# One attention and expert-routing layer on one core: softmax sums from a column of ones, a router maximum as a bias, and a new order of steps

## The reference

```python
h = _L0_tok_ref(x, ...)                  # gated recurrence: z, f, o from two-tap convolutions
h = h + _L0_attn_ref(_layernorm(h), ...) # attention to 39 offsets (0..32, 48, 64, 96, 128, 192, 256)
h = h + _L0_ffn_ref(_layernorm(h), ...)  # router over 64 experts, top 2, capacity 128, shared GELU FFN
# attention, for each head:
scores = where(valid, q . k[n - offset] * (1 + scale) / 4 + bias, -inf)
attn = softmax(scores, axis=offset)
out = sum over offsets of attn * v[n - offset]
# router: probs = softmax(logits); the two largest; a token's gate is the sum of the kept ones
```

## Time and profile before

| | us |
|---|---|
| median of 3 runs (lowest, highest) | 430.35 (429.63, 431.35) |
| span of the profiled execution, first to last instruction | 428.5 |
| what the median has beside that span | 1.85 |
| mean granted PE clock over the span (share of full speed) | 0.997 |

### The profile page before, as it was taken

One profiled execution on the slowest core, in us unless ns is written; L12 is line 12 of the kernel. 1 busy time (PEld: TensorE's weight loads), 2 busy tenths in 40 slices (PEclk: granted clock), 3 DMA queues, 4 the chain that ended last, 5 costly groups with the idle time before them and its releaser, 6 DMA issues.

```text
span 428.5 us, 12683 instructions
## 1 busy us (share of the span) xinstructions
PE 405.3 (95%) x4554; PEld 278.6 (65%) x4554; DVE 380.8 (89%) x873; ACT 323.1 (75%) x728; POOL 372.7 (87%) x391
## 2 busy tenths in 40 slices
PE   8788789999999999999999999999999999998884
PEld 5444364776757676776767677676767675766763
DVE  2586999899999999999999999999999999999563
ACT  3756768879687877968687887868788796859773
POOL 7696999999989989898998989898998999997611
PEclk9999999999999999999999999999999999999998
DMA  6530866462737265372826446273735547265500
GB/s 230 192 105 2 200 165 182 105 174 62 200 88 183 79 154 150 86 207 61 198 71 149 143 120 186 55 201 82 178 95 129 158 109 190 65 182 127 133 13 24
DMA packets 78702, 56.08 MB, mean 131 GB/s; under 512 B 28304, under 2 KB 71344, under 8 KB 78512
## 3 DMA queue, kind: packets, MB, share of 16 engines
q1 hardware_dynamic: 78640, 55.28, 48.1%
HBM read 35.56 MB, written 19.70 MB: 129 GB/s over the span
## 4 chain that ended last, share of the span: by engine, by line
PE 74%; POOL 8%; issue 3%; DVE 3%; DMA 2%; ACT 1%; SPq 0%; POOLq 0%; DVEq 0%; ACTq 0%
PE bank L456 18%; PE bank L552 9%; PE bank L529 8%; PE bank L432 6%; PE bank L405 5%; PE bank L489 5%; PE bank L406 5%; PE bank L477 4%; POOL prod L1724 4%; POOL fprod L1709 3%; PE bank L468 3%; PE bank L521 2%; PE bank L505 2%; PE bank L440 2%; PE bank L424 1%
## 5 line engine op out<-in xcount | busy, mean ns | idle before, releaser
L1724 POOL TENSOR_TENSOR prod<-q,k 128x1448 f32<-128x1448 f32 (+2 forms) x48 | 145.6, 3053 | 17.4 <-ACT k L865 13.0
L1247 DVE SCALAR_TENSOR_TENSOR prod<-bank,par,k 128x1432 f32<-128x1432 f32 (+4 forms) x80 | 134.9, 1693 | 0.0
L456 PE MATMUL bank<-prod,ew 128*32 128x374 f32 (+7 forms) x1024 | 84.3, 467 | 2.4 <-ACT gate L872 1.0
L1709 POOL TENSOR_TENSOR fprod<-q,k 128x326 f32<-128x326 f32 (+6 forms) x112 | 79.0, 742 | 0.0
L456 PEld LDWEIGHTS bank<-prod,ew 128*32 128x32 f32 x1024 | 31.4, 110 | 44.9 <-issue 37.9
L972 ACT ACTIVATE hid<-bank,par 128x374 f32<-128x374 f32 x64 | 36.3, 575 | 23.8 <-PE bank L529 22.0
L799 ACT ACT_TABLE_LOAD x40 | 51.3, 1283 | 1.4 <-PEq L1944 0.7
L529 PE MATMUL bank<-x,par 128*128 128x374 f32 x128 | 48.4, 484 | 2.0 <-ACT x L925 2.0
L552 PE MATMUL bank<-par,hid 128*128 128x128 f32 x384 | 47.9, 276 | 0.0
L552 PEld LDWEIGHTS bank<-par,hid 128*128 128x128 f32 x384 | 45.9, 192 | 2.5
L405 PE MATMUL bank<-xT,par 128*128 128x374 f32 x96 | 40.9, 508 | 1.2 <-DVE mixin L1200 0.6
(11 more groups left out here) (123 smaller groups left out, 873.6 us busy)
## 6 DMA issues: line engine op xcount, KB each, us to landing
band<-band_scratch SPq DMA_DIRECT2D x16, 768.0 KB, 5.5
band_scratch<-attn SPq DMA_DIRECT2D x64, 180.4 KB, 3.0
vnear<-v_scratch SPq DMA_DIRECT2D x48, 192.0 KB, 3.1
v<-v_scratch SPq DMA_DIRECT2D x32, 192.0 KB, 4.1
v_scratch<-vtok SPq DMA_DIRECT2D x16, 192.0 KB, 3.0
xT<-x_dram SPq DMA_DIRECT2D x16, 187.5 KB, 3.4
vfar<-v_scratch SPq DMA_DIRECT2D x16, 128.0 KB, 3.3
out_dram<-osb SPq DMA_DIRECT2D x16, 128.0 KB
```

What stands on the lines that cost most here:

```text
L456: done = mm(home(f"s{c}")[32 * g:32 * g + 32, lo:N], ew[:, COLS[c] + j, :], src[:, j, lo:N], start=first or only, stop=last or only)
L1247: v.scalar_tensor_tensor(bass.AP(prod[c][:, :, :].tensor, first * N + lo, [[CW * N, 128], [N, w], [1, N - lo]]), home("q")[:, lo:N].unsque ...
L1709: last = g.tensor_tensor(fprod[:, i, o:N], q[q_.s][:, o:N], k[q_.s][:, KPAD:KPAD + N - o], ALU.mult)
L1724: g.tensor_tensor(bass.AP(prod[c][:, :, :].tensor, first * N + lo, [[CW * N, 128], [N, w], [1, N - lo]]), q[q_.s][:, lo:N].unsqueeze(1).br ...
```

## The change

Every value row gets one more slot per head, which holds 1.0 (`VH = 17`, a row of `VD = 136`). It is carried by the same DMAs, near and far products, far sums and `attend`, so the sum of the weights stands beside the weighted values in `pv` after `attention_sum`. `softmax_sum` goes; `softmax_rcp` now reads the sums from `pv` between `attention_sum` and `attention_norm`. `softmax_exp` exponentiates only the three far columns that POOL needs (24 x 3 in place of 24 x 39). `router_subtract` goes; DVE negates the maximum (`least`) in `route_picks`, and `router_exp` takes it as its bias, from the logits themselves.

The rest is order. Five PSUM tiles change banks (`k`, `ts0`, `tb1`, `tb2`, `x2b`), and all five queues are written anew. PE's turn now begins later in the same cycle, so that its indices are one larger for the same work. In ACT's turn the table changes four times in place of two.

```diff
-        HOME = dict(z=4, f=1, o=7, ht=2, xb=0, q=3, k=7, v=1, g=5, s0=4, s2=5, s1=5, ts0=4, ts1=3, ts2=5, tb0=1,
-                    tb1=0, tb2=6, pv=1, ot=1, op=0, x2b=4, lg=6, pos=7, up0=0, up1=5, up2=7, up3=4, dn=6)
+        HOME = dict(z=4, f=1, o=7, ht=2, xb=0, q=3, k=0, v=1, g=5, s0=4, s2=5, s1=5, ts0=7, ts1=3, ts2=5, tb0=1,
+                    tb1=7, tb2=4, pv=1, ot=1, op=0, x2b=0, lg=6, pos=7, up0=0, up1=5, up2=7, up3=4, dn=6)
```

The head of PE's turn and its last lines, and a piece of the order before its loop:

```diff
+                if a6:
+                    turn_band(a6, 2, ("s0", a5))
+                    turn_band(a6, 1, ("ts0", a5))
+                    attend(a6, 0, ("tb0", a6), head=True)
+                    attend(a6, 2)
+                    attend(a6, 1)
+                if a7:
+                    turn_x2(a7, ("k", a4))
+                if a2:
+                    convolve(a2, 2, ("tb1", a6))
+                if a7:
+                    up(a7, 3, ("tb2", a6), head=True)
+                    logits(a7, ("dn", a8))
+                    up(a7, 0, ("x2b", a7))
+                if a6:
+                    turn_o(a6, ("pv", a6))
+                if a1:
+                    convolve(a1, 0, ("up3", a7), ("tb2", a6), head=True)
...
+                if a3:
+                    project(a3, "k", ("xb", a3), head=True)
+                    project(a3, "q", ("ts1", a4))
...
+            score(seq[0], 0, 3, last=True)
+            turn_scores(seq[0], 1, ("q", seq[0]))
+            project(seq[1], "k", ("xb", seq[1]), head=True)
+            project(seq[1], "q", ("ts1", seq[0]))
+            turn_scores(seq[0], 0, ("o", seq[2]))
             score(seq[0], 2, 0, ("s1", seq[0]), first=True)
-            score(seq[0], 0, 3, last=True)
             score(seq[0], 2, 1, last=True)
-            turn_scores(seq[0], 1, ("q", seq[0]))
-            turn_scores(seq[0], 0, ("s0", seq[0]))
-            project(seq[1], "k", ("o", seq[2]), head=True)
-            project(seq[1], "q", ("ts1", seq[0]))
```

PE, sequence 15 near the end:

```diff
-            up(seq[14], 3, ("x2b", seq[14]), head=True)
             attend(seq[15], 0, ("tb0", seq[15]), head=True)
             attend(seq[15], 2)
             attend(seq[15], 1)
...
+            up(seq[14], 3, ("tb2", seq[15]), head=True)
```

ACT, the exponentials and its turn:

```diff
-                A(ex[:, :, :], sc[:, :, :], ACT.Exp).then_inc(ex_ready, 1)
+                A(ex[:, :, :].rearrange("p o r -> p r o"), sc[:, :, 1:2 * (NFAR - NEAR):2], ACT.Exp).then_inc(ex_ready, 1)
...
-                act.wait_ge(lsub_ready, q_.b + 1)
+                act.wait_ge(least_ready, q_.b + 1)
...
-                    done = A(exr[:, t, :], lsub[:, t, :], ACT.Exp, accum_out=smr[:, t:t + 1])
+                    done = A(exr[:, t, :], lg[:, t, 0:EXPERTS], ACT.Exp, bias=least[:, t:t + 1], accum_out=smr[:, t:t + 1])
...
+                    softmax_far(a4)
+                    softmax_dense(a4)
                 if a6:
                     norm2_back(a6)
                 if a4:
-                    softmax_dense(a4)
-                    softmax_far(a4)
+                    softmax_exp(a4)
                 if a1:
                     tanh_o(a1)
...
+                if a6:
+                    router_exp(a6)
                 if a0:
                     tanh_z(a0)
                     tanh_f(a0)
-                if a6:
-                    router_exp(a6)
+                if a3:
+                    open_gate(a3)
+                if a2:
+                    norm1_ln(a2)
...
+                if a4:
+                    band_copy(a4, 0)
+                if a2:
+                    copy_k(a2)
+                    copy_q(a2)
+                if a4:
+                    band_copy(a4, 2)
+                    band_copy(a4, 1)
```

DVE:

```diff
-            def softmax_sum(q_):
-                dve.wait_ge(ex_ready, q_.b + 1)
-                v.tensor_reduce(sm[:, :], ex[:, :, :], AX.X, ALU.add).then_inc(sm_ready, 1)
...
+                sums = bass.AP(home("pv")[:, :].tensor, WIN, [[512, 128], [HALF, TT * 2], [1, PAIRS]])
+                v.reciprocal(rs[q_.s][:, :].rearrange("p (r i) -> p r i", i=PAIRS), sums).then_inc(rs_ready, 1)
...
+                v.tensor_scalar(least[:, :], m8[:, :, 0], -1.0, None, ALU.mult).then_inc(least_ready, 1)
```

POOL, near the end:

```diff
-            router_subtract(seq[12])
+            far_products(seq[15], 0)
+            far_products(seq[15], 1)
             kept_mask(seq[12])
-            far_products(seq[15], 0)
             kept_weights(seq[12])
-            far_products(seq[15], 1)
```

More of the change, by code:

```diff
@@ L354, in _ @@
-            load_x(seq[3])
[L355 to L363, removed]
-            pipeline(sp, turn, range(5, 17))
+                a1, a5, a6, a8 = at(1), at(5), at(6), at(8)
+                if a6:
+                    read_band(a6)
+                if a5:
+                    write_values(a5)
@@ new lines, in turn @@
+                if a1:
+                    load_x(a1)
+                if a8:
+                    store_out(a8)
+                if a5:
+                    read_near(a5)
+                    read_far(a5)
+                    read_values(a5)
+                    write_attn(a5)
+            load_x(seq[3])
+            pipeline(sp, turn, range(5, 17))
+            read_band(seq[11])
+            write_values(seq[12])
+            read_near(seq[12])
+            read_values(seq[12])
+            read_far(seq[12])
@@ L578, in turn @@
[L578 to L590, removed]
@@ new lines, in _ @@
+            turn_band(seq[12], 1, ("ts0", seq[13]))
+            turn_x2(seq[11], ("k", seq[14]))
+            attend(seq[12], 0, ("tb0", seq[12]), head=True)
+            attend(seq[12], 2)
+            attend(seq[12], 1)
+            up(seq[11], 3, ("tb2", seq[12]), head=True)
+            logits(seq[11], ("dn", seq[10]))
+            up(seq[11], 0, ("x2b", seq[11]))
+            turn_o(seq[12], ("pv", seq[12]))
+            up(seq[11], 2, ("tb1", seq[12]))
+            up(seq[11], 1, ("ts2", seq[13]))
@@ new lines, in _ @@
+            out_project(seq[12], ("up0", seq[11]))
+            value_project(seq[14], ("ot", seq[12]))
+            project(seq[14], "g", ("up1", seq[11]))
+            down(seq[11], 0, ("lg", seq[11]), head=True)
+            down(seq[11], 1)
+            positions(seq[11], ("up2", seq[11]))
+            turn_h(seq[15], ("ht", seq[14]))
+            down(seq[11], 2)
+            score(seq[14], 1, 0, ("g", seq[14]), first=True)
+            score(seq[14], 1, 1)
+            score(seq[14], 0, 1, ("up3", seq[11]), first=True)
@@ L1501, in _ @@
             score_subtract(seq[0])
-            products(seq[1], 0, 1, head=True)
+            stats1(seq[2])
             near_values(seq[0])
@@ L1869, in _ @@
             far_sum(seq[14], 5)
-            carry(seq[15])
+            carry(seq[14])
             far_sum(seq[15], 1)
-            router_subtract(seq[13])
-            kept_mask(seq[13])
-            kept_weights(seq[13])
             far_values(seq[15], 4)
```

849 lines of the change are left out of this document (431 added, 418 removed).

## The result

The changed kernel takes 445.23 us (443.76 to 447.24), the kernel before in the same session 430.85 (429.63 to 431.45): 1.0353 times as long, 95% interval 1.0316 to 1.0390. The forecast was 425.5, so the sign was wrong. The profiled execution has a span of 441.9, 13.4 more than before.

A forecast was written before the change was run, and what follows sets the result against it. PE was taken to bound the middle turns, so gains come only at the ends: 428.5 - 2.6 - 2.8 + 0.55 = 423.65 us of span, 4.85 less, hence 430.35 - 4.85 = 425.5 us; range 422.5 to 431.0.

The forecast's parts named there:

- One tiny negation: DVE's turn: the added negation, given no duration; DVE would reach at most 23.8 us, below PE's 24.54.
- The write of the band now ends SP's turn; its reader is most of a turn away: SP's turn: the band's later write was taken as harmless and given no cost.
- These cover it: DVE's turn: nine instructions after finish would hide near loads of 3.1 us from near_values, larger rows included; no cost.
- ACT's order: ACT's middle turn: 21.3 us of work with four switches fits beside PE, slack 0.00 and 0.15 at two places.
- The rival on ACT: Middle turns: ACT's queue sets the turn; at 0.75 us per turn the time is 433.2; chance 0.18.
- rival of a switch held for twice its row: ACT's table switches: its turn becomes 26.4 us, 1.9 more in ten turns, 444.5 in all; chance 0.01.
- Only one end arrives: Start or end: the gain of 2.6 or 2.8 us is missing, giving 428.1 to 428.3; chance 0.18.
- The middle turn: Repeated turns: PE stays busy; 0.05 us of waiting per turn, attend's columns included, 0.55 lost over 11 turns.
- The start: First sequences: POOL no longer idles 3.50 us before sequence 1's products, so sequence 2's products start 2.6 us earlier.
- The end: Last sequences: POOL's last far products come earlier (2.46 us left) and the last chain gains 0.33: 2.8 us.
- The masks' later place: positions moves behind two down, so keep and kept_mask come later; PE has other work meanwhile, costed at nothing.

The follow-up runs named there:

- e3: The change with SP's store_out last in its turn and, in SP's written-out end, each band written and read ahead of the next value rows: 431.21 us.
- e7: The kernel before with one unused tensor_scalar negation of three elements added per sequence ahead of the router's memset: 447.29 us.
- e9: The change with SP's written-out end reordered (band ahead of next value rows) and the negation as a tensor_reduce, SP's turn left alone: 428.19 us.
- e5: e3 with the negation made by a tensor_reduce in place of a tensor_scalar: 427.99 us.
- e6: The change, SP's queue unmended, with the negation made by a tensor_reduce: 438.57 us.
- e8: e5 with router_exp moved behind both tanh and the opened gate, so two table loads a turn in place of four: 427.53 us.
- e10: e8 with router_exp of sequence 14 moved behind the second norm of sequence 15 in ACT's end section: 431.38 us.

## Why the prediction was wrong

- **"One tiny negation" is the term that was mis-sized.** The prediction counted it among DVE's small gains and gave it no duration, while DVE had 0.7 us to spare. It takes up to 2.77 us, since it ends with POOL's running instruction (the rows of the change, e3, e7). In the change this is worth 445.23 - 438.57 = 6.6 us. In the turns from 110 to 210 us it takes up to 0.6, and five later ones take 1.1 to 2.8: there POOL's order is written out, and its third local product starts later against DVE (at 286.57 in the rows above, behind a sum and a carry that begin at 284.60). None of the DVE instructions of before near that place is of this kind, but its set-up has one, and it shows the price: `hbias`, a `tensor_scalar` of 12 elements, took 1.24 us and ended 0.03 behind a POOL instruction (below). The Trainium skill has the rule: its page "SBUF — State Buffer", section "Who interferes with whom", says that a `tensor_scalar` can, if its operands meet certain conditions, take the pair of ports that VectorE (DVE) and GpSimd (POOL) share, that the later of the two blocks until the other's whole instruction ends, and that a `tensor_reduce` on trn2 never contends. The traces agree in both: ends 0.02 to 0.04 us behind POOL's, and 145 to 158 ns for the `tensor_reduce`. I had not weighed that rule.

```profile
4.06 1.38 POOL L1668 MEMSET v<- 128x1536 f32 x1
...
4.23 1.24 DVE L1187 TENSOR_SCALAR hbias<-par 128x12 f32<-128x12 f32 x1 [3.28 <-DMA par<-params_dram]
```

- **"The write of the band now ends SP's turn; its reader is most of a turn away" is the step that failed.** It holds in the repeated turns. In the written-out end section the write of band 12 stands behind a wait for the next value rows, and the read of band 13 behind two stores; I had read the lists there for PE, POOL and DVE, not for SP. By itself this is 445.23 - 435.63 = 9.6 us. With both causes gone the time is 445.23 - 428.19 = 17.0 us less.
- **"These cover it"** (nine DVE instructions over the near loads) was wrong as it stood, since loads landed after up to 6.3 us and `near_values` waited 5.4 in all. By itself it costs little (e9 against e5, 0.2; 0.8 in the stretch of e6); it hurt while DVE was held as well.
- **ACT's order was laid out rightly.** Its turn has 21.5 us of work (21.3 forecast), and taking two of its four loads away changed nothing that can be told (e8, 0.5). The drain that the Trainium skill's page "ScalarE: Activation LUTs", section "What ACT_TABLE_LOAD costs", adds to each switch does not show here either: in the undisturbed turn a load starts at 203.77, takes 1.28, and the next function starts at 205.07. The rival on ACT, with 0.18, was the wrong one. That the rival of a switch held for twice its row named 444.5, near the measured 445.23, is chance: a load takes 1283 ns. "Only one end arrives" had the band's DMAs late, but priced them at the missing 2.8; no rival named SP's order in the end section as a loss, or the negation.
- **The middle turn, 24.59 forecast, is 24.62.** The wider `attend` is the part that shows: 28.1 us in all against 26.1, 0.12 per sequence, above the bound of 0.10.
- **The start, 2.6 forecast, gave 2.6** in this execution, in part by luck; in the kernels with the same start it lies between 1.5 and 3.8. POOL reaches the products of sequence 2 not 2.65 but 3.83 earlier: its first product comes 0.10 earlier instead of 0.47 later, and the far block before them takes 5.57 us, not 6.07 + 0.38, since a product of far weights and values fell from 877 to 653 ns although it is wider. POOL's middle turn is 21.64, not the 22.25 forecast. Why PE gained only 2.6 of the 3.83 is open.
- **The end, 2.8 forecast, gives 1.9** once SP is mended: from the mark of sequence 13 to the end e9 takes 83.26 us, the kernel before 85.13. POOL's last far product ends 5.8 us earlier than before in e9 (379.79 against 385.55), about 5.5 forecast, and 2.9 nearer to that mark, 2.98 forecast. So what is missing lies behind it: from there to the end e9 takes 44.04 us and the kernel before 42.98, 1.06 more where the forecast had 0.19. Why is open.
- **The masks' later place** cost nothing, as said: POOL waits 31.0 us for `kept` instead of 7.4, and e5's turns are full all the same.

With the two mends the profiled execution of e9 spans 423.8 us, where the sum gave 423.65. That is the fastest of its twelve runs, and the terms only add up to the same: 3.8 less at the start (2.6 forecast), 1.9 less at the end (2.8), 1.0 more between (0.55). The median of e9 lies 2.7 above the forecast; part of that may be PE's clock at the end, below, but no run measured it by itself.

## What to carry to other kernels

Read the order of every queue in the written-out prologue and end as well as in the repeated turn: a wait put ahead of a ready write there was worth 9.6 us. Price a new instruction by what may hold it and not by its size: three elements on VectorE cost 17 us where another form of the same step cost nothing. An instruction of the same kind anywhere in the trace, set-up included, can show it beforehand. A late transfer that shows in the list of waits need not be a cause; take the wait away alone, and then with the other causes gone, before it is given a price.

## What the runs showed of the hardware

PE's granted clock can fall after idle time, as in the turn of 28.4 us above, and so before the last FFN too. Busy time by stretch of e10, where PE had 1.34 us of work in the 5 us before, and of e8, where it had no such pause:

```profile
410.00:415.00 5.00, 1.34 (x6) 0.54 (x4) 2.04 (x7) 3.33 (x9) 0.59 (x1) 0.88 0.00 0
415.00:420.00 5.00, 5.00 (x12) 3.09 (x13) 1.72 (x12) 1.48 (x3) 0.00 (x0) 0.50 0.14 40
```

```profile
412.00:417.00 5.00, 4.02 (x26) 2.74 (x27) 2.19 (x15) 4.60 (x8) 0.00 (x0) 1.00 0.14 40
417.00:424.00 7.00, 2.58 (x24) 2.39 (x22) 2.37 (x9) 1.87 (x7) 1.14 (x2) 1.00 0.08 24
```

At 0.50, the level of 1.2 GHz, a matmul of the last `up` steps takes 0.83 us instead of 0.48. Their gelus still take 0.57 each, but start 1.24 us apart instead of 0.63, which adds to the loss of e10. The spread of the runs goes with the clock: of e9's twelve, the six with a mean clock of 0.995 or more took 425.6 to 428.2 us, the six below 428.2 to 429.9.
